# Other distances, by pads and one offset, between the stationary and the moving tiles of a two-layer transformer kernel

## What is computed

```python
x = x + _L0_xattn_ref(_layernorm(x, axis=-1), ctx_4096, ctx_4096, mask, L0_xattn_wq, ..., 0)
x = x + _L0_ffn_ref(_layernorm(x, axis=-1), L0_ffn_w_gate, L0_ffn_w_up, L0_ffn_w_down)
x = x + _L1_xattn_ref(_layernorm(x, axis=-1), ctx_4096, L1_xattn_Wq, ..., q_norm_w, k_norm_w)
x = x + _L1_ffn_ref(_layernorm(x, axis=-1), gamma, beta, w1, b1, w3, b3)
```

## Time and profile before

| | before |
|---|---|
| median of 3 runs | 1532.07 us (1531.17 to 1535.59) |
| the profiled execution's own time | 1531.07 us |
| its span, first to last instruction | 1529.3 us |
| matmuls on TensorE (PE) busy | 1475.2 us, 96% |
| weight loads (PEld) busy | 1276.0 us, 83% |
| VectorE / ScalarE / GpSimd busy | 950.2 / 597.5 / 564.3 us |

### The profile page before, as it was taken

One profiled execution on the slowest core, in us unless ns is written; L12 is line 12 of the kernel. 1 busy time (PEld: TensorE's weight loads), 2 busy tenths in 40 slices (PEclk: granted clock), 3 DMA queues, 4 the chain that ended last, 5 costly groups with the idle time before them and its releaser, 6 DMA issues.

```text
span 1529.3 us, 28684 instructions
## 1 busy us (share of the span) xinstructions
PE 1475.2 (96%) x11536; PEld 1276.0 (83%) x11536; DVE 950.2 (62%) x1983; ACT 597.5 (39%) x1434; POOL 564.3 (37%) x468
## 2 busy tenths in 40 slices
PE   6899999999999998999899999999999999999986
PEld 5788888888888876887798899898899989889973
DVE  7666665665666675666866456455655645565588
ACT  4313222222222234442355353444435344443556
POOL 4535354443536423652134122222312222231258
PEclk9999999999999999999899999999999999999998
DMA  7111020111112003320112011110101011010201
GB/s 198 42 29 50 21 69 29 42 30 41 43 29 65 8 20 97 80 60 21 42 29 70 1 43 29 28 43 21 50 1 42 29 29 43 14 57 1 80 5 56
DMA packets 84302, 64.45 MB, mean 42 GB/s; under 512 B 7280, under 2 KB 71024, under 8 KB 84176
## 3 DMA queue, kind: packets, MB, share of 16 engines
q1 hardware_dynamic: 83600, 62.47, 14.2%
q10 hardware_dynamic: 576, 0.20, 0.1%
HBM read 60.56 MB, written 2.10 MB: 41 GB/s over the span
## 4 chain that ended last, share of the span: by engine, by line
PE 47%; DVE 2%; POOL 1%; issue 1%; ACT 0%; DVEq 0%; ACTq 0%; POOLq 0%
PE att_proj L70 35%; PE att_att L800 4%; PE att_sco L758 4%; PE att_att L775 2%; PE att_proj L722 1%; PE att_sco L737 1%; POOL ffn_y L476 0%; DVE ffn_top L428 0%; DVE ffn_y L470 0%; POOL x_rows L414 0%; PE att_att L242 0%; DVE ffn_y L424 0%; DVE stats L383 0%; DVE x_rows L1053 0%; ACT ffn_y L435 0%
## 5 line engine op out<-in xcount | busy, mean ns | idle before, releaser
L148 POOL TENSOR_TENSOR att_w_lo<-w_raw,att_w_hi 128x512 fp32r<-128x512 f32 x160 | 206.7, 1317 | 179.5 <-ACT att_w_hi L143 172.0
L1416 POOL TENSOR_TENSOR att_probs<-att_probs,att_total 128x512 f32<-128x512 f32 x64 | 82.8, 1294 | 455.8 <-DVE att_total L1037 341.7
L70 PE MATMUL att_proj<-att_w_hi,kv_hi 128*128 128x256 f32 x768 | 223.4, 291 | 10.2 <-DVE kv_lo L260 10.2
L70 PE MATMUL att_proj<-att_w_hi,kv_lo 128*128 128x256 f32 x768 | 218.3, 284 | 0.0
L70 PE MATMUL att_proj<-att_w_lo,kv_hi 128*128 128x256 f32 x768 | 218.3, 284 | 0.0
L70 PE MATMUL att_proj<-kv_hi,att_w_hi 128*128 128x512 f32 x512 | 207.6, 406 | 1.5 <-DVE kv_lo L251 1.5
L70 PE MATMUL att_proj<-att_w_hi,att_o_hi 128*128 128x512 f32 x512 | 205.0, 400 | 1.9 <-issue 1.9
L70 PE MATMUL att_proj<-kv_lo,att_w_hi 128*128 128x512 f32 x512 | 201.8, 394 | 0.0
L70 PE MATMUL att_proj<-kv_hi,att_w_lo 128*128 128x512 f32 x512 | 201.5, 393 | 0.0
L70 PE MATMUL att_proj<-att_w_lo,att_o_hi 128*128 128x512 f32 x512 | 199.8, 390 | 0.0
L70 PE MATMUL att_proj<-att_w_hi,att_o_lo 128*128 128x512 f32 x512 | 199.5, 390 | 0.0
(11 more groups left out here) (167 smaller groups left out, 2740.2 us busy)
## 6 DMA issues: line engine op xcount, KB each, us to landing
w_raw<-in_wq SPq DMA_DIRECT2D x64, 256.0 KB, 2.9
w_raw<-in_wo SPq DMA_DIRECT2D x64, 256.0 KB, 2.8
w_raw<-in_wk SPq DMA_DIRECT2D x16, 256.0 KB, 3.0
w_raw<-in_wv SPq DMA_DIRECT2D x16, 256.0 KB, 3.3
w_raw<-in_gate_t SPq DMA_DIRECT2D x10, 256.0 KB, 2.9
w_raw<-in_up_t SPq DMA_DIRECT2D x10, 256.0 KB, 3.1
w_raw<-in_down_t SPq DMA_DIRECT2D x10, 256.0 KB, 3.0
spare<-in_ctx_t SPq DMA_DIRECT2D x4, 512.0 KB, 5.7
```

Source lines behind the costliest of these rows:

```text
L70: ins = eng.matmul(out, a, b, start=(first and n == 0), stop=(last and n == 3 * len(terms) - 1))
L148: eng.tensor_tensor(self.lo[:, chunk], self.raw[:, n % RAW_SLOTS], raw(self.hi[:, chunk]), ALU.subtract)\
L1416: eng.tensor_tensor(probs[:, u % 2, 0:n], probs[:, u % 2, 0:n], total[:, u % 2, 0:n].unsqueeze(2).broadcast_to([P, n, KL]), ALU.mult)\
```

## The change

Pads are declared ahead of some tiles, one pad gets larger, and `share` places `gu_hi` and `gu_lo` 64 words further in the memory that they share with `kv0`. No instruction is added, removed or moved; with line numbers left out, the order of every engine reads the same before and after, waits included. What changes is the addresses. The distances of the large matmuls, stationary to moving, modulo 512 bytes, with the number of matmuls from the loops of the code:

| stage | matmuls | before | after |
|---|---|---|---|
| first attention, key/value jobs (256 columns) | 768 | 0 | 64 |
| first attention, queries | 768 | 0 | 64 |
| first attention, output projection | 768 | 0 | 256 |
| first feed-forward, gate and up | 528 | 0 | 256 |
| first feed-forward, down | 176 | 0 | 128 |
| second attention, key/value jobs (256 columns) | 1536 | 0 | 256 |
| second attention, queries | 768 | 256 | 0 |
| second attention, output projection | 768 | 0 | 128 |

Together they are 6080. Of the plain fp32 matmuls, the weighted values go from 0 to 256 (first attention) and 128 (second), and the transposes change as their inputs move; the scores stay at 0.

```diff
@@ attention
         k_rows = sb("k_rows", [P, NBH * KL // P, HD])
+        sb("o_pad", [P, 64 if rope else 32])
         o_hi, o_lo = (sb(n, [P, GROUP, NBH, S], F32R) for n in ("o_hi", "o_lo"))
@@ FfnWeights.share
-        n = 4 * KT * P
-        self.gu_hi, self.gu_lo = (flat_lo[:, i * n:(i + 1) * n].rearrange("p (a b k n) -> p a b k n", a=2, b=2, k=KT)
-                                  for i in range(2))
+        n, ahead = 4 * KT * P, 64
+        self.gu_hi, self.gu_lo = (
+            flat_lo[:, i * n + ahead:(i + 1) * n + ahead].rearrange("p (a b k n) -> p a b k n", a=2, b=2, k=KT)
+            for i in range(2))
@@ int_ffn
+        sb("hid_pad", [P, 32])
         hid = sb("hid", [P, CF, TOK], F32R)
@@ build
+                scope.enter_context(nc.sbuf_tensor("att0_w_pad", [P, 16], F32))
                 first.place(nc, scope)
@@ build
-            scope.enter_context(nc.sbuf_tensor("kv1_pad", [P, 112], F32, side="right"))
+            scope.enter_context(nc.sbuf_tensor("kv1_pad", [P, 176], F32, side="right"))
```

## The result

The changed kernel takes 1537.7 us (median of 9 runs, 1536.1 to 1539.3) against 1532.7 (9 runs, 1530.5 to 1535.6) for the kernel before: a ratio of 1.0033, 95% interval 1.0024 to 1.0041, so 5.0 us slower. The forecast was no change.

The account below looks back on a forecast made before the run. The prediction took the time as a sum over TensorE's matmuls, put every stage's change at 0, and so forecast 1532 us from the profiled 1531.07 and a median 1.0 higher, range 1525 to 1544.

Parts of the forecast that it names:

- What bounds the kernel: Whole kernel: TensorE's matmuls busy 1475.2 of 1529.3 us, so 1 ns on each of 6080 large matmuls is 6.1 us.
- The first witness: Last matmul of a first-attention query job: 388 ns with no weight load beside it, so the extra 10 ns need no load.
- the term 0 at 64 and 128: First attention's key/value jobs and queries, down, second attention's output projection: 2480 matmuls, step taken as unchanged, 0 us.
- The second witness: Second attention's queries, already at 256, step 226 ns as gate and up at 0, so 0 and 256 are the same.
- the carry-over: Stages going from 0 to 256 or 256 to 0 in both attentions, gate and up: step unchanged, 0 us.
- The third witness: Plain fp32 matmuls at 0 and 96 both take 275 ns, so weighted values and transposes change by 0; called weaker.
- The rule on the ports: TensorE reads moving and stationary operands through two independent ports, so loading the next tile costs the running matmul nothing: 0.
- Rival C: At 64 or 128 load and moving stream collide: up to 4.3 ns on 2480 matmuls, +11 us, 1543 us; chance 0.18.
- Its point of decision: The slowdown on the 2480 matmuls at 64 and 128 decides from 4.6 / 2480 = 1.9 ns a matmul on.
- Rival B: At 64 and 128 the 10 ns an fp32r matmul carries over bf16 go: -25 us, 1507 us; chance 0.12.
- The 1532 us: Whole kernel: profiled 1531.07 us plus 0, forecast for a median 1.0 higher.
- "same": Whole kernel: 1527.5 to 1536.7 us, as a measurement can tell about 0.3% from no change.

Follow-up runs that it names:

- only_256: Kernel before plus only the change's edits that move stages from 0 to 256 or 256 to 0: 1531.5 us, ratio 0.9998.
- split64: Kernel before with own tiles for key/value weights: those jobs at 64 in both attentions, all else 0 or 256; 1527.2 us, ratio 0.9967.

## Why the prediction was wrong

**What bounds the kernel** held. Time is a sum over matmuls; the weight loads (1275.9 against 1276.0 us) and the other engines didn't change.

**The first witness failed**, and with it the term 0 at 64 and 128. Its row was read rightly: that matmul lasts 388 ns with no load beside it. What failed is the step from there, "a distance to the tile that the load reads cannot take them away" and so "what isn't there beside a load is not made by it". It took the length of one lone matmul at distance 0 for what any distance does to a row of matmuls, and no row of a large matmul stood at 64 or 128. In its place the runs showed that the step follows the distance: at 64 and 128 it is 232 to 233 ns for 512 columns in place of 226.7, and 117.7 in place of 120 for the first attention's key/value jobs. The four stages put at 0 made -1.4, +3.1, +0.6 and +3.8 us.

Lone matmuls don't show why. After shows the same one at 64, again with no load until 3.9 us later (order of time, then the group of it alone, from 45.83 us on):

```profile
45.27 0.39 PE L70 MATMUL att_proj<-kv_hi,att_w_lo 128*128 128x512 f32 x1
45.50 0.40 PE L70 MATMUL att_proj<-kv_lo,att_w_hi 128*128 128x512 f32 x1
49.44 0.48 PE L776 MATMUL att_att<-ident,att_probs 128*128 128x128 f32 x1 [3.54 <-POOL att_probs L1417]
...
45.27 0.19 PEld L70 LDWEIGHTS att_proj<-kv_lo,att_w_hi 128*128 128x128 f32 x1
49.44 0.29 PEld L776 LDWEIGHTS att_att<-ident,att_probs 128*128 128x128 f32 x2 [3.98 <-POOL att_probs L1417]
...
L70 PE MATMUL att_proj<-kv_lo,att_w_hi 128*128 128x512 f32 x1 | 0.4, 397 | 0.0
```

397 ns in place of 388 looks like an effect of the distance. But before has a last matmul of a job of the same length at distance 0, in the first attention's output projection, with no load beside it either (order of time, then the group from 557.12 us on):

```profile
556.64 0.19 PEld L70 LDWEIGHTS att_proj<-att_w_lo,att_o_hi 128*128 128x128 f32 x1
556.87 0.40 PE L70 MATMUL att_proj<-att_w_lo,att_o_hi 128*128 128x512 f32 x1
557.83 0.31 PEld L775 LDWEIGHTS att_att<-ident,att_probs 128*128 128x128 f32 x3 [1.00 <-POOL att_probs L1416]
...
L70 PE MATMUL att_proj<-att_w_lo,att_o_hi 128*128 128x512 f32 x1 | 0.4, 397 | 0.0
```

So at one distance the modelled length of a lone matmul is 388 or 397 ns, and it decides nothing: whether the extra needs a load beside it stays open.

**The second witness held.** 0 and 256 are the same for 512 columns, and the carry-over to the other stages too: `only_256` 0.9998, none of the stages that it moves off by more than 0.2 us.

**The third witness** held for what it spoke of: weighted values and transposes in plain fp32, at their new distances, took the same time (275 and 285 ns a matmul, 272 for the second attention's transposes), and all steps outside the large matmuls together changed by -0.3 us. It said nothing about fp32r.

**The rule on the ports** (the Trainium skill, "TensorE: Matmul & The Clock Gate", "Step-by-step: what each phase is for") gave the same term 0. The result doesn't show that the ports share anything, but what the prediction drew from it, that the places of the two operands can't matter, is wrong here: 226.7 against 233.3 ns at the same granted clock.

**Rival C**, given 0.18, came on three of its four stages, in sign and place; its mechanism, a load and a moving stream that meet in the memory, isn't shown. Its price of 4.3 ns was too low for a settled stretch (233.3 - 226.7 = 6.6) and near the stage means (3.1 / 768 = 4.0 ns in queries, 3.8 / 768 = 4.9 in the output projection, 0.6 / 176 = 3.4 in down), in part because the first steps of a job are longer than 226.7 already before. Its sum was too high because the place named as the worst, the first attention's key/value jobs, went the other way: -1.4 us in place of 768 x 4.3 = +3.3. The argument there (a load in a step of 120 ns has little slack) was about loads, and the loads didn't get longer. Its point of decision held: 1.9 ns a matmul over 2480, and what came is 6.1 / 2480 = 2.5 ns without down's low clock.

**Rival B** failed for 512 columns, where no distance was below 226.7, and was partly right for 256 columns: at 64 a step loses 2 to 7 of its 120 ns.

**The 1532 us** missed the 1537.7 that was measured, which lies in the range and 1.0 us outside "same".

## What to carry to other kernels

Read what a matmul's step is at the distance between its moving and stationary tiles that the kernel has, and try others with a pad: for fp32r at 512 columns multiples of 256 bytes were best by up to 3%, for 256 columns in two pieces 64 was better than 0 by 2 to 6%. Tiles that feed two kinds of jobs tie their distances together; splitting them (`split64`) let each stand at its own best. And a stall that is there without its supposed cause doesn't exclude that what it costs depends on where things lie: only a row in which that quantity differs can say so.

## What the hardware showed that was not expected

- Four settled steps are multiples of about 6.67 ns: 226.7 is 34 of them, 233.3 is 35, 120 is 18 and 113.3 is 17. Others are not (229 and 117.7, and the single steps that repeat in threes), so a grid to which each start is held isn't shown. Sums over three matmuls are: 687 ns is 103 of them, 353 is 53.
- At 512 columns the step depends on the distance with a period of 256 bytes and reacts to a single word (232.5 ns at 4 bytes). What was tried of distances other than 0 and 256 was slower, 192, 240 and 448 least. For 256 columns several other distances were faster than 0.
- At one and the same distance (64) the 256-column jobs have two settled paces, 113.3 and 117.7 ns, kept for a whole stretch. Which of the two a stretch takes was not settled.
